# The V projection moved into the first LayerNorm loop, and the softmax reciprocal replaced by Ln and Exp, in a transformer layer on eight cores

## What is computed

```python
x = x + attn(layernorm(x), W_qkv, W_o)
x = x + ffn(layernorm(x), ...)

def attn(x, W_qkv, W_o):
    q, k, v = heads of einsum('bsd,ed->bse', x, W_qkv)
    q, k = rope(q), rope(k)
    scores = einsum('bhqd,bhkd->bhqk', q, k) / sqrt(64)
    attn = softmax(where(causal, scores, -inf))
    return einsum('bsd,ed->bse', einsum('bhqk,bhkd->bhqd', attn, v), W_o)
```

## Time and profile before

| | us |
|---|---|
| median of two timed runs | 6523.15 |
| lowest, highest | 6501.34, 6544.97 |
| profiled execution | 6577.09 |
| its span (core 7, the slowest) | 6575.6 |
| its fastest core (core 3) | 6498.7 |

### The profile page before, as it was taken

How to read it: one execution, slowest core, us unless ns; L and a number is a source line. 1 busy time by engine, 2 the same in 40 slices (tenths; PEclk the granted TensorE clock), 3 DMA queues, 4 the chain that set the end, 5 groups by cost and what they waited for, 6 DMA issues and landing times. The chain is left out here.

```text
span 6575.6 us, 44751 instructions; the slowest of 8 cores (6498.7 to 6575.6 us)
## 1 busy us (share of the span) xinstructions
PE 4366.0 (66%) x11412; PEld 1076.1 (16%) x11412; DVE 2274.4 (35%) x2561; ACT 1711.9 (26%) x1991; POOL 1428.5 (22%) x1736
## 2 busy tenths in 40 slices
PE   0067888884336888887325788888532688888833
PEld 0022111121112211112002211111201221111200
DVE  1342333323444233323344333323344423333234
ACT  0001444430000344441000044444000014444200
POOL 0072000002347000000335400000123810000033
PEclk9997555555569655556558855555655965555655
DMA  5310000010021000002021000000103100000101
GB/s 146 114 28 15 1 0 0 1 45 23 36 86 29 0 1 0 0 0 67 0 83 47 21 1 0 0 1 7 60 7 109 23 13 1 0 0 1 60 8 61
DMA packets 151759, 180.28 MB, mean 27 GB/s; under 512 B 89948, under 2 KB 110556, under 8 KB 151012
## 3 DMA queue, kind: packets, MB, share of 16 engines
q1 hardware_dynamic: 151526, 177.43, 8.7%
HBM read 133.36 MB, written 44.04 MB: 27 GB/s over the span
## 5 line engine op out<-in xcount | busy, mean ns | idle before, releaser
L576 ACT ACTIVATE PT<-pss,ecol_s 128x1024 bf16<-128x1024 f32 x1280 | 1426.5, 1115 | 1669.1 <-PE pss L558 1663.0
L528 DVE RECIPROCAL rb<-psb 64x512 f32<-64x512 f32 x256 | 857.6, 3350 | 2231.6 <-PE psb L519 2231.6
L558 PE MATMUL pss<-qkT 64*128 64x512 bf16 x2560 | 1316.5, 616 | 8.1 <-PEq L68 8.1
L497 PE MATMUL pso<-PT,v 128*65 128x512 bf16 (+3 forms) x2560 | 1201.2, 565 | 16.7 <-POOL PT L591 16.6
L591 POOL TENSOR_SCALAR_AFFINE_SELECT PT<-PT 128x128 bf16<-128x128 bf16 x1024 | 274.9, 292 | 3300.6 <-ACT PT L576 3299.9
L519 PE MATMUL psb<-lr,ones_s 1*64 1x512 f32 x512 | 494.4, 1065 | 404.8 <-ACT lr L512 404.8
L382 PE MATMUL psq<-u1T,wqk 128*128 128x512 bf16 x2048 | 489.6, 383 | 238.7 <-DVE t1b L395 221.9
L776 PE MATMUL psz<-t,ones_s 128*1 128x512 f32 x256 | 228.4, 1046 | 490.4 <-DVE t L768 490.4
L497 PEld LDWEIGHTS pso<-PT,v 128*65 128x65 bf16 x2560 | 274.6, 140 | 1130.4 <-issue 1097.5
L328 PE MATMUL ptr<-ident_s,u1b 128*128 128x128 bf16 x512 | 64.7, 306 | 589.2 <-DVE u1b L316 589.2
L408 POOL TENSOR_TENSOR t2b<-qks,ropeB_s 128x512 f32<-128x512 f32 x256 | 324.5, 1268 | 396.0 <-DVE t1b L395 359.5
(11 more groups left out here) (96 smaller groups left out, 2205.9 us busy)
## 6 DMA issues: line engine op xcount, KB each, us to landing
xb<-x SPq DMA_DIRECT2D x64, 512.0 KB, 3.5
xr<-x SPq DMA_DIRECT2D x64, 512.0 KB, 3.6
out<-x2o SPq DMA_DIRECT2D x64, 512.0 KB, 2.6
wqk<-wqk_b SPq DMA_DIRECT2D x64, 256.0 KB, 3.0
cbuf_f<-wqk SPq DMA_DIRECT2D x16, 512.0 KB, 4.5
wvb<-wv_b SPq DMA_DIRECT2D x32, 256.0 KB, 4.4
wob<-wo_b SPq DMA_DIRECT2D x32, 256.0 KB, 4.7
wqk_b<-cbuf_b SPq DMA_DIRECT2D x16, 256.0 KB, 2.8
```

The lines of the kernel that those rows point to most:

```text
L497: e.matmul(pso[i_hqb % 2][0:65, sigma:512], vsb[:, j * NH * 66 + h * 66: j * NH * 66 + h * 66 + 65], PT[:, sl4 * 512 + sigma: sl4 * 512 + ...
L528: e.reciprocal(rb[sl][:, :], psb[sl][0:64, :])
L558: e.matmul(pss[sl2][:, (jj % 2) * 512: (jj % 2) * 512 + 512], qkT[hb:hb + 64, kcol + jj * 128: kcol + (jj + 1) * 128], qkT[hb:hb + 64, qco ...
L576: e.activation(PT[:, slot0 * 512: slot0 * 512 + 1024], pss[sl2][:, :], AF.Exp, bias=self.ecol[:, 1:2], scale=0.125) \
```

## The change

Three edits.

1. The V stage goes. Its 16 steps (`plan_v`) are written out inside the LayerNorm loop: after tile t comes the V projection of tile t - 1, and the last one behind the loop. `wvb` is allocated and loaded at the start of the block, ahead of the first x tile.
2. In the tail of the softmax ScalarE takes the Ln of the row of sums before the broadcast, and Exp with scale -1 of the broadcast, in place of VectorE's reciprocal.
3. `crow4` is no longer kept for the whole program but loaded at the start of each `p3`, which frees the room that `wvb` needs beside `u1T`.

```diff
@@ p1
             u1T = self.sb(sc, f"u1T_{s}", [128, DC * S], BF16)
+            wvb = self.sb(sc, f"wvb{s}", [128, DC * D], BF16)
...
+            for c in range(DC):
+                self.add("sync", lambda e, c=c: e.dma_start(
+                    out=wvb[:, c * D:(c + 1) * D], in_=self.wv_b[c])
+                    .then_inc(self.s_ldw2.h, 16))
...
+                def plan_v(t):
+                    sl = t % 2
+                    w_ev2 = b_vev + t - 1 if t >= 2 else 0
+                    w_u1T = b_ev + t + 1
+                    def _vmm(e, t=t, sl=sl, w=v_wv, w2=w_ev2, wu=w_u1T,
+                             first=(t == 0)):
+                        if first:
+                            e.wait_ge(self.s_ldw2.h, w)
+                        e.wait_ge(self.s_u1T.h, wu)
+                        if w2:
+                            e.wait_ge(self.s_vev.h, w2)
+                        for c in range(DC):
+                            for nb in range(2):
+                                ins = e.matmul(
+                                    psv[sl][:, nb * 512:(nb + 1) * 512],
...
+                    self.add("vector", lambda e, d=dstap, sr=srcap, w=v_vmm,
+                             w2=wv_first: (
+                        e.wait_ge(self.s_misc.h, w2) if w2 else None,
+                        e.wait_ge(self.s_vmm.h, w),
+                        e.tensor_copy(d, sr).then_inc(self.s_vev.h, 1)))
...
                         e.tensor_copy(d, sr).then_inc(self.s_u1T.h, 1)))
+                    if t >= 1:
+                        plan_v(t - 1)
+                plan_v(NT - 1)
...
-            with ExitStack() as scc:
-                wvb = self.sb(scc, f"wvb{s}", [128, DC * D], BF16)
...
@@ plan_tail
-                self.add("scalar", lambda e, sl=i_hqb % 2, w=w_pv: (
+                c1 = self.s_ch.inc()
+                self.add("scalar", lambda e, sl=i_hqb % 2, w=w_pv, c1=c1: (
                     e.wait_ge(self.s_pvmm.h, w),
                     e.copy(lrow[sl][:, :], pso[sl][64:65, :])
+                     .then_inc(self.s_ch.h, 1),
+                    e.wait_ge(self.s_ch.h, c1),
+                    e.activation(lrow[sl][:, :], lrow[sl][:, :], AF.Ln)
                      .then_inc(self.s_lrow.h, 1)))
...
+                self.add("scalar", lambda e, sl=i_hqb % 2, w=v_bc: (
+                    e.wait_ge(self.s_bc.h, w),
+                    e.activation(rb[sl][:, :], psb[sl][0:64, :], AF.Exp,
+                                 scale=-1.0).then_inc(self.s_rstd.h, 1)))
...
-                    e.wait_ge(self.s_bc.h, w),
-                    e.reciprocal(rb[sl][:, :], psb[sl][0:64, :])
-                     .then_inc(self.s_ch.h, 1),
-                    e.wait_ge(self.s_ch.h, c1),
+                    e.wait_ge(self.s_rstd.h, w),
                     e.tensor_mul(d, pso[sl][0:64, :], rb[sl][:, :])
@@ p3
+            crow4 = self.sb(sc, f"crow4_{s}", [1, 4 * D], F32)
+            self.add("sync", lambda e: e.dma_start(
+                out=crow4[:, :], in_=self.din["crow"][:, 0:4 * D])
+                .then_inc(self.s_ldw2.h, 16))
```

More of the change, by code:

```diff
@@ L151, in phase0 @@
             self.s_c0.inc(16)
[L152 to L155, removed]
         casts = []
@@ L262, in p1 @@
                      .then_inc(self.s_misc.h, 1))
+            for c in range(DC):
+                self.add("sync", lambda e, c=c: e.dma_start(
+                    out=wvb[:, c * D:(c + 1) * D], in_=self.wv_b[c])
+                    .then_inc(self.s_ldw2.h, 16))
+                self.s_ldw2.inc(16)
+            v_wv = self.s_ldw2.n
             with ExitStack() as sca:
@@ L271, in p1 @@
                        for i in range(2)]
+                psv = [self.ps(sca, f"psv{s}_{i}", [128, 1024], F32)
+                       for i in range(2)]
                 b_u1 = self.s_u1.n
@@ L274, in p1 @@
                 b_ev = self.s_u1T.n
+                b_vmm = self.s_vmm.n
+                b_vev = self.s_vev.n
+                def plan_v(t):
[13 more added lines that the diff above has]
+                                    psv[sl][:, nb * 512:(nb + 1) * 512],
+                                    u1T[:, c * S + t * 128: c * S + (t + 1) * 128],
+                                    wvb[:, c * D + nb * 512: c * D + (nb + 1) * 512],
+                                    start=(c == 0), stop=(c == DC - 1),
+                                    skip_group_check=True)
+                        ins.then_inc(self.s_vmm.h, 1)
+                    self.add("tensor", _vmm)
+                    v_vmm = self.s_vmm.inc()
+                    dstap = (vsb[:, t * NH * 66:(t + 1) * NH * 66]
+                             .rearrange("p (h c) -> p h c", c=66)[:, :, 0:64])
+                    srcap = psv[sl][:, :].rearrange("p (h c) -> p h c", c=64)
+                    wv_first = v_vset if t == 0 else 0
+                    self.add("vector", lambda e, d=dstap, sr=srcap, w=v_vmm,
[3 more added lines that the diff above has]
+                        e.tensor_copy(d, sr).then_inc(self.s_vev.h, 1)))
+                    self.s_vev.inc()
                 for t in range(NT):
@@ L417, in p1 @@
                         self.s_qkT.inc()
-            with ExitStack() as scc:
-                wvb = self.sb(scc, f"wvb{s}", [128, DC * D], BF16)
[L421 to L458, removed]
-                    self.add("vector", lambda e, d=dstap, sr=srcap, w=v_vmm,
-                             w2=wv_first: (
-                        e.wait_ge(self.s_misc.h, w2) if w2 else None,
-                        e.wait_ge(self.s_vmm.h, w),
-                        e.tensor_copy(d, sr).then_inc(self.s_vev.h, 1)))
-                    self.s_vev.inc()
@@ L522, in plan_tail @@
                 v_bc = self.s_bc.inc()
+                self.add("scalar", lambda e, sl=i_hqb % 2, w=v_bc: (
+                    e.wait_ge(self.s_bc.h, w),
+                    e.activation(rb[sl][:, :], psb[sl][0:64, :], AF.Exp,
+                                 scale=-1.0).then_inc(self.s_rstd.h, 1)))
+                v_e = self.s_rstd.inc()
                 dst = attnT[(h % 2) * 64:(h % 2) * 64 + 64,
                             (h // 2) * S + qb * 512:(h // 2) * S + qb * 512 + 512]
-                c1 = self.s_ch.inc()
-                self.add("vector", lambda e, sl=i_hqb % 2, d=dst, w=v_bc, c1=c1: (
-                    e.wait_ge(self.s_bc.h, w),
-                    e.reciprocal(rb[sl][:, :], psb[sl][0:64, :])
-                     .then_inc(self.s_ch.h, 1),
-                    e.wait_ge(self.s_ch.h, c1),
+                self.add("vector", lambda e, sl=i_hqb % 2, d=dst, w=v_e: (
+                    e.wait_ge(self.s_rstd.h, w),
                     e.tensor_mul(d, pso[sl][0:64, :], rb[sl][:, :])
```

13 lines of the change are left out of this document (7 added, 6 removed).

## The result

The changed kernel takes 6719.30 us (median of 11 runs, 6704.51 to 6792.48) against 6517.07 us for the kernel before (10 runs). The ratio is 1.0307, with a 95% interval of 1.0285 to 1.0329: slower by 3.1%, where 3.3% was forecast (6740 us). One of the 11 runs, that of 6792.48 us, fell into a slower state with the cores of one die at a lower clock, and the ratio leaves it out. The profiled execution has a span of 6730.0 us on its slowest core, which is now core 2. The medians of its two dies (cores 0 to 3 and 4 to 7) are 6714.4 and 6703.6 us; before, they were 6502.2 and 6549.0.

A forecast was written before the change was run, and what follows sets the result against it. Attention was taken as bound by a chain PE, ACT copy, PE. Core 7: 6577 + 176 + 6 = 6759 us; core 1's clock: 6507 + 176 + 40 = 6723 us; forecast 6740 us, range 6650 to 6850 us.

The forecast's parts named there:

- The Ln: Softmax tail, ACT between copy and broadcast: 0.63 us plus 0.10 for the step, uncovered, 256 x 0.73 = +187 us.
- The Exp: Softmax tail, ACT behind the broadcast: 0.59 us, hidden with 0.4 us to spare, cost 0 on the path.
- The tail: Softmax tail in attention, new Ln and Exp in place of the reciprocal: +176 us together.
- The removed reciprocals: Softmax tail on DVE: 256 of 3.35 us give nothing back except at sequence ends, -2.65 x 4 = -11 us.
- Rival 6: First exp of attention: its set lacks Ln, each tail switches twice, 512 x 1.28 us = +657, 7397 us; chance 0.03.
- The LayerNorm loop: V groups inside the loop leave DVE idle for each group: period 10.8 us, 171.8 against 90.0 us per sequence.
- the sum: Total over the kernel: core 7 6577 + 176 + 6, a core like core 1 6507 + 176 + 40 us.
- D: LayerNorm loop, the V matmul group up to the V copy: 5.3 us, bounds 3.6 and 7.0, -95 and +95 us.
- tile 0: First tile of the LayerNorm loop: 10.1 us, its u1b taking 5.70 instead of 0.81 us beside the memset of v.
- The loads: Start of the block: wvb ahead of x makes the first tile some 5 us late; taken as 0, at most 20 us.
- The third level of the clock: V groups in the LayerNorm loop: 13/16 of the clock might cost 0.4 us per group, 64 x 0.4 = 26 us.

The follow-up runs named there:

- e5: The changed kernel with the Exp of the broadcast row computed twice on ACT, first result unused: 6740.06 us, ratio 1.0344 to the kernel before.
- e1: The kernel before with the new softmax tail alone, the V projection keeping its own stage: 6691.78 us, ratio 1.0292 to the kernel before.
- e3: The changed kernel with the Ln reading the row of sums straight from PSUM, without the copy: 6546.54 us, ratio 1.0067 to the kernel before.
- e2: The changed kernel with the old tail (reciprocal on VectorE), so only the V projection is moved: 6537.60 us, ratio 1.0052 to the kernel before.
- e4: The changed kernel with VectorE copying V one tile later in the LayerNorm loop: 6464.29 us, ratio 0.9934 to the kernel before.
- e9: e4 with the tail cut in two, broadcast, Exp and product written out one pair later: 5970.37 us, ratio 0.9155 to the kernel before.

## Why the prediction was right, step by step

**The Ln.** Forecast 0.63 us and 0.10 for the step, PE's wait from 404.8 to about 590 us. Measured 0.628 us, and the wait is 588.5. The groups of the changed kernel:

```profile
L513 ACT ACTIVATE lr<-lr 1x512 f32<-1x512 f32 x256 | 160.8, 628 | 23.8 <-ACT lr L510 0.4
L526 ACT ACTIVATE rb<-psb 64x512 f32<-64x512 f32 x256 | 151.0, 590 | 583.9 <-PE psb L520 583.9
```

**The Exp.** Forecast 0.59 us, hidden, with 0.4 us to spare. Measured 0.590 us with 0.43 us before the next exp, and e5 laid a second one into the same gap. Attention was to take about 864 us and takes 863.5. The tail was priced at +176 us; e1 shows 2.92% of 6506, which is 190 us, with 18 us to either side; the four attention stages together grew from some 3288 to 3462 us, by 174.

**The removed reciprocals.** They gave nothing back beyond the ends of the sequences, as forecast: DVE's busy time fell from 2274.4 to 1396.7 us (878 us), and attention got longer. e3 isolates them better: with the Exp in place of the reciprocal and PE's wait for the row back at 407.1 us, the four attention stages took 3280 to 3282 us against 3287 to 3289 before, 7 us less in all where 11 were forecast.

**Table loads.** Rival 6 is false. The changed kernel still has 4 table loads at the exp of attention, one per sequence, and none at the Ln or the Exp of the tail:

```profile
L578 ACT ACT_TABLE_LOAD x4 | 5.1, 1283 | 784.1 <-PE pss L560 784.1
```

The rule of the Trainium skill (ScalarE: Activation LUTs, "Table sets: the hidden batching unit") that Exp and Ln exist in one set agrees with this trace. Its figure of about 2.7 us for a switch, which the prediction quotes, no run here shows; the load itself takes 1.28 us in this row, the price that rival 6 used.

**The LayerNorm loop.** The mechanism was forecast as it stands in the timeline above: VectorE idle behind u1T until the group of the tile before ends. e2 puts the V half at +0.5%, or 34 us, between the +6 of the sum for a core like core 7 and the +40 for one like core 1. The term that was off is D, the time from the start of the group to the copy of V. Forecast was 5.3 us, derived from one start of a rested TensorE less a share of the transposes. Measured is 4.81 us in the quicker tile shown and 5.82 in the slower one. Six of the eight cores had the quicker pattern nearly throughout: their 14 periods per sequence average 10.4 us, against 10.8 forecast, and their four stretches from the first u1b to the first QK matmul add up to 640 to 644 us. On cores 2 and 3 the periods average 10.9 and the stretches add up to 672.6 and 672.1. The QK stages that follow became 1.6 us shorter each on core 7, where 1.8 were forecast.

The forecast for these stretches was 4 x 171.8 = 687 us, and the 14 us that core 2 lies under it are not owed to D. The sum had 10.1 us for tile 0 with its slow u1b; measured are 5.1 to 5.3, 20 us less over four sequences, because the wait has moved ahead of the first u1b (see the loads). Without this core 2 took some 6 us more than forecast, and the quicker cores about 25 less.

That the median lies within 21 us of the forecast is in part luck. The forecast was the middle between two cores. For one like core 7 it had 6759 us, and core 7 has a span of 6699.2: some 35 us of the difference lie in the output projection and the feed-forward part, which no edit was meant to speed up, and which took 1584 us on core 7 before and 1550 now, the same as on core 1 before. For one like core 1 it had 6723, and core 1 has 6705.0. The slowest core is now core 2, which was not among the two, and it is slowest for a pattern of the clock that the forecast did not have.

**The loads.** wvb ahead of x made tile 0 late as expected, and most of that was no loss, since before the change the first u1b was stretched beside the memset:

```profile
1863.02 14.18 POOL L257 MEMSET v<- 128x16896 bf16 x1 [0.81 <-POOLq L68]
...
1877.82 0.81 DVE L357 TENSOR_SCALAR u1b<-xb,mv,rs 128x1024 bf16<-128x1024 f32 x1 [2.07 <-ACT rs L350]
```

From the start of the memset to the end of the first u1b it is 15.6 us here, and was 14.7, with a u1b of 0.81 instead of 5.70 us. On core 2 the four sequences have 15.0 to 15.8 us, 0.7 us more per sequence than the 14.7 of before; on core 7 one has 16.8.

**The third level of the clock.** The prediction left open whether a V group with rests around it can get the third level that the Trainium skill describes (TensorE: Matmul & The Clock Gate, "Seeing it yourself"). It can: the last matmuls of the slower group above ran at 0.81, those of the quicker one at 1.00. The prediction's estimate for it, 0.4 us per group, holds: the weight loads of the slower group follow each other every 0.26 us in that stretch and those of the quicker group every 0.22, so 8 matmuls cost between 0.3 and 0.4 us more (an estimate from these spacings). The rest of the 1.01 us between the two groups is the later rise, some 8 matmuls at 0.427 us against 5. The same section of the Trainium skill says that this limit takes the whole die to 13/16 of the clock. This trace does not agree, and the measurement decides: read in steps of 1 us from 1950 to 1998, the upper level was 0.81 on cores 2 and 3 and 1.00 on the other six, cores 0 and 1 of the same die among them.

## What to carry to other kernels

A cheaper instruction is worth nothing if it shortens an engine that nobody waits for, and a short one is dear if it lengthens the chain between two instructions of the engine that sets the pace: 0.72 us more in each of 256 tails cost 2.9%, while 256 reciprocals of 3.35 us had cost 7 us in all. Before work is moved into a gap, look at who reads its result and where that reader stands in its own queue; an in-order engine that reads too early turns the gap into its own idle time, and a copy one tile later made 3.1% loss into 0.7% gain. The largest prize lay in neither edit but in the order: a row that is needed two blocks later was waited for on the spot, and one pair of other work laid over that wait gave 7.6% (e4 to e9).

## What the runs showed that was not expected

The same loop on the same core ran in two patterns of the clock, which the two groups above show from inside. In the changed kernel, on core 2, the mean granted clock from the first u1b to the first QK matmul was 0.85 in the first sequence and 0.66 in the second (the rows of the stretches above), for 160.3 and 174.9 us, with identical instructions. In the quicker pattern the period settles at 10.24 us. In the slower one it goes round in threes, 10.88, 11.94 and 11.29 us, over and over, 11.4 on average. In the stretch from 1900 to 2000 us cores 2 and 3 had 0.66 and the six others 0.83 or 0.84 at the same time:

```profile
1900.00:2000.00 100.00, 56.37 (x208) 24.50 (x210) 36.98 (x54) 4.47 (x18) 0.00 (x0) 0.66 0.14 44
```

```profile
1900.00:2000.00 100.00, 53.83 (x234) 25.28 (x235) 39.92 (x59) 4.98 (x20) 0.00 (x0) 0.83 0.18 53
```

A loop whose bursts on TensorE are separated by rests of 4.8 us can thus settle at either, and the cost of a burst is not one number. What decides between the two, the length of the stay at 0.50 and the level that follows it, was not tried.
